# The last tile's way out: quantisation on two engines, down product in two column halves, stores on two queues

## The reference

```python
    x = x + ffn(cond(x, length, log_dt, C, log_A_real, A_imag, D), w_gate, w_up, w_down, ...)

    def cond(u, ...):                        # a convolution, written with FFTs
        u_m = u * mask[:, None, :]
        y = irfft(rfft(u_m, n=1024) * rfft(kernel, n=1024))[..., :512]
        return (y + u_m * D[:, None]) * mask[:, None, :]

    def ffn(x, ...):
        xq = int4_quant(x)                   # mean |x| of a row, round, clip to -8..7
        gate = bitlinear(xq, w_gate, s_gate) # 512 -> 1376
        up = bitlinear(xq, w_up, s_up)       # 512 -> 1376
        gate = jnp.square(jax.nn.relu(gate))
        inter = int8_quant(up * gate)        # max |x| of a row, x * 127 / (gamma + eps), round
        return bitlinear(inter, w_down, s_down)   # 1376 -> 512
```

## Time and profile before

| | |
|---|---|
| median of 3 runs | 215.71 us (215.28 to 215.75) |
| the profiled execution | 215.85 us |
| its span, from the first to the last instruction | 214.1 us |
| mean granted TensorE clock | 0.991 of full speed (2.4 GHz) |
| TensorE, VectorE, ScalarE busy | 84%, 78%, 54% of the span |
| the last add ends, the last store is issued | 210.7 us, 211.2 us |

### The profile page before, as it was taken

The page is one execution under the profiler, slowest core; times in us unless marked ns, Lnnn a source line. Parts: engine busy times, 40 slices in busy tenths (PEclk is TensorE's granted clock), DMA queues, the critical chain, the costliest instruction groups (busy, mean ns, idle before and its releaser), DMA issues.

```text
span 214.1 us, 3425 instructions
## 1 busy us (share of the span) xinstructions
PE 180.8 (84%) x1136; PEld 97.0 (45%) x1136; DVE 168.0 (78%) x457; ACT 115.0 (54%) x184; POOL 11.0 (5%) x29
## 2 busy tenths in 40 slices
PE   1011679499969999999999999999999999998882
PEld 1011576345524554545454545454545545454340
DVE  5999886579987979696968787786969696969841
ACT  2277949829943645545463728282736455464410
POOL 4034502000000000000000000000000000000000
PEclk9999999969999999999999999999999999999999
DMA  3999849426999676667483949484757667070722
GB/s 79 370 385 307 283 122 336 140 74 170 168 202 227 189 162 195 146 169 175 139 213 118 221 116 225 114 243 91 227 116 203 126 190 150 15 164 5 165 49 49
DMA packets 43488, 36.61 MB, mean 171 GB/s; under 512 B 29872, under 2 KB 29952, under 8 KB 43472
## 3 DMA queue, kind: packets, MB, share of 16 engines
q1 hardware_dynamic: 42816, 34.93, 62.6%
q10 hardware_dynamic: 336, 1.41, 1.9%
q0 software_dynamic: 320, 0.06, 0.3%
HBM read 25.27 MB, written 4.28 MB: 138 GB/s over the span
## 4 chain that ended last, share of the span: by engine, by line
PE 71%; DVE 11%; ACT 8%; issue 3%; DMA 3%; SPq 2%; DVEq 0%
PE down_ps L607 18%; PE gate_ps L566 16%; PE up_ps L571 15%; PE conv_ps L481 15%; PE tr_act_ps L471 2%; DMA int_gate<-int_down 2%; ACT int_up L642 2%; PE tr_dve_ps L494 1%; ACT int_gate L649 1%; ACT int_down L642 1%; ACT int_up L649 1%; DVE inter L1046 1%; PE tr_dve_ps L536 1%; DMA c_in<-in_L_cond_C_dram 1%; SPq L358 1%
## 5 line engine op out<-in xcount | busy, mean ns | idle before, releaser
L705 ACT ACTIVATE g<-gate_ps,gu_scale 128x416 f32<-128x416 f32 (+2 forms) x48 | 30.5, 636 | 66.5 <-issue 55.6
L1046 DVE SCALAR_TENSOR_TENSOR inter<-up_ps,gu_scale,g 128x416 f32<-128x416 f32 (+2 forms) x48 | 33.1, 690 | 18.3 <-ACT g L708 18.2
L566 PE MATMUL gate_ps<-gate_t,q_t 128*128 128x416 bf16 (+2 forms) x192 | 45.2, 358 | 1.1 <-DVE q_t L985 1.1
L571 PE MATMUL up_ps<-up_t,q_t 128*128 128x416 bf16 (+2 forms) x192 | 45.5, 360 | 0.0
L607 PE MATMUL down_ps<-down_t,i_t 128*128 128x512 bf16 (+1 forms) x176 | 40.7, 380 | 2.2 <-DVE i_t L1073 1.0
L481 PE MATMUL conv_ps<-toep,x_t 128*64 128x512 f32 (+3 forms) x256 | 39.1, 449 | 0.1
L1050 DVE TENSOR_REDUCE imax<-inter 128x1 f32<-128x416 f32 (+2 forms) x48 | 30.3, 631 | 1.6
L708 ACT ACTIVATE g<-g 128x416 f32<-128x416 f32 (+2 forms) x48 | 28.1, 586 | 1.5
L571 PEld LDWEIGHTS up_ps<-up_t,q_t 128*128 128x128 bf16 x192 | 18.8, 98 | 18.5 <-issue 0.2
L607 PEld LDWEIGHTS down_ps<-down_t,i_t 128*128 128x128 bf16 (+1 forms) x176 | 17.0, 98 | 22.4 <-DVE i_t L1073 1.4
L481 PEld LDWEIGHTS conv_ps<-toep,x_t 128*64 128x64 f32 x256 | 17.2, 139 | 20.7 <-issue 16.8
(11 more groups left out here) (170 smaller groups left out, 165.4 us busy)
## 6 DMA issues: line engine op xcount, KB each, us to landing
toep<-k_back SPq DMA_DIRECT2D x16, 512.0 KB, 5.1
x_in<-in_x_dram SPq DMA_DIRECT2D x32, 128.0 KB, 2.8
x_res<-in_x_dram SPq DMA_DIRECT2D x32, 128.0 KB, 4.0
out_dram<-o_sb SPq DMA_DIRECT2D x32, 128.0 KB, 2.5
raw_gate<-in_L_ffn_w_gate_dram SPq DMA_DIRECT2D x1, 1536.0 KB, 7.2
raw_up<-in_L_ffn_w_up_dram SPq DMA_DIRECT2D x1, 1536.0 KB, 13.9
raw_down<-in_L_ffn_w_down_dram ACTq DMA_DIRECT2D x1, 1376.0 KB, 6.9
raw_down<-in_L_ffn_w_down_dram SPq DMA_DIRECT2D x1, 1376.0 KB, 9.0
```

Of the source, the lines that this page charges most:

```text
L566: mm = pe.matmul(gate_ps[bank][:, 0:cn], q_t[p][:, i, :], gate_t[:, i, c0:c0 + cn], start=(i == 0), stop=(i == KB - 1))
L571: mm = pe.matmul(up_ps[bank][:, 0:cn], q_t[p][:, i, :], up_t[:, i, c0:c0 + cn], start=(i == 0), stop=(i == KB - 1))
L705: nc.scalar.activation(g2[bank][:, 0:cn], gate_ps[bank][:, 0:cn], ACT.Relu, scale=gu_scale[p][:, 0:1]).then_inc(relu_done, 1)
L1046: v.scalar_tensor_tensor(out=inter[:, c0:c0 + cn], in0=up_ps[bank][:, 0:cn], scalar=gu_scale[p][:, 1:2], in1=g2[bank][:, 0:cn], op0=ALU.mu ...
```

## The change

It concerns the last tile alone, and the add of the one before:

- ScalarE quantises the 608 columns, VectorE the 768 as before; both wait for `iscale`, for which there is a new semaphore `iscale_ready`.
- `keep_clock(8)` becomes `keep_clock(2)`.
- The shares of the copies change hands: VectorE copies the first six blocks, ScalarE the other five, in two instructions.
- The down product runs twice over the eleven blocks, for output columns 0 to 255 into `conv_ps` and for 256 to 511 into `up_ps[0]`. It waits for VectorE's copy, and before block seven for ScalarE's. It no longer waits for tile 14's add.
- VectorE adds tile 14 behind its copy, and then each half as it is done (`add_out`).
- SyncE stores the first half in two DMAs (64 rows of 1 KB each) and then half 0 of the second; ScalarE issues the DMA of the second's other 64 rows.

```diff
+        LAST = [(conv_ps, slice(0, L // 2)), (up_ps[0], slice(L // 2, L))]
 # SyncE
-                if k >= 2:
+                if k == T + 1:
+                    sp.wait_ge(out_ready, T)
+                    for half in range(2):
+                        sp.dma_start(in_dram(out, T - 1, half)[:, LAST[0][1]],
+                                     o_sb[p][half_rows(half), LAST[0][1]]).then_inc(stored[p], 16)
+                    sp.wait_ge(out_ready, T + 1)
+                    sp.dma_start(in_dram(out, T - 1, 0)[:, LAST[1][1]],
+                                 o_sb[p][half_rows(0), LAST[1][1]]).then_inc(stored[p], 16)
+                elif k >= 2:
 # TensorE, turn_last
-                keep_clock(8)
+                keep_clock(2)
 # TensorE, down
                 if k == T:
-                    pe.wait_ge(it_act_copied, 1)
+                    pe.wait_ge(it_dve_copied, T)
+                    for bank, cols in LAST:
+                        for c in range(IB):
+                            if c == IT_SPLIT:
+                                pe.wait_ge(it_act_copied, 1)
+                            r = P if c < IB - 1 else IR
+                            mm = pe.matmul(bank[:, 0:L // 2], i_t[0:r, c, :], down_t[0:r, c, cols],
+                                           start=(c == 0), stop=(c == IB - 1))
+                        mm.then_inc(down_done, 1)
+                    return
 # ScalarE
                 if k == T:
-                    act.wait_ge(it_turned, 1)
+                    act.wait_ge(iscale_ready, 1)
+                    act.wait_ge(it_loaded, 16 * (T - 1))
+                    cut = slice(IT_SPLIT * P, I)
+                    nc.scalar.activation(inter_q[:, cut], inter[:, cut], ACT.Copy,
+                                         scale=iscale[:]).then_inc(inter_quant, 1)
+                    act.wait_ge(it_turned, 2)
                     act.wait_ge(down_done, T - 1)
-                    nc.scalar.copy(i_t[:, 0:IT_SPLIT, :].rearrange("p c t -> p (c t)"),
-                                   tr_act_ps[:, 0:IT_SPLIT * P // 2].bitcast(I16)).then_inc(it_act_copied, 1)
+                    nb = IB - 1 - IT_SPLIT
+                    nc.scalar.copy(i_t[:, IT_SPLIT:IB - 1, :].rearrange("p c t -> p (c t)"),
+                                   tr_dve_ps[:, 0:nb * P // 2].bitcast(I16))
+                    nc.scalar.copy(i_t[0:IR, IB - 1, :], tr_dve_ps[0:IR, nb * P // 2:(nb + 1) * P // 2].bitcast(I16)
+                                   ).then_inc(it_act_copied, 1)
+                    act.wait_ge(out_ready, T + 1)
+                    act.dma_start(in_dram(out, T - 1, 1)[:, LAST[1][1]],
+                                  o_sb[1][half_rows(1), LAST[1][1]]).then_inc(stored[1], 16)
 # VectorE
+                def add_out(n, bank, cols, done):
+                    q = n % 2
+                    dve.wait_ge(down_done, done)
+                    dve.wait_ge(res_loaded[q], 32 * (n // 2 + 1))
+                    wait(dve, stored[q], 32 * (n // 2))
+                    v.scalar_tensor_tensor(out=o_sb[q][:, cols], in0=bank[:, 0:cols.stop - cols.start],
+                                           scalar=oscale[q][:], in1=x_res[q][:, cols],
+                                           op0=ALU.mult, op1=ALU.add).then_inc(out_ready, 1)
...
                 if k == T:
-                    dve.wait_ge(it_turned, 2)
+                    dve.wait_ge(it_turned, 1)
                     dve.wait_ge(down_done, T - 1)
-                    nb = IB - 1 - IT_SPLIT
-                    v.tensor_copy(i_t[:, IT_SPLIT:IB - 1, :].rearrange("p c t -> p (c t)"),
-                                  tr_dve_ps[:, 0:nb * P // 2].bitcast(I16))
-                    v.tensor_copy(i_t[0:IR, IB - 1, :], tr_dve_ps[0:IR, nb * P // 2:(nb + 1) * P // 2].bitcast(I16)
-                                  ).then_inc(it_dve_copied, 1)
+                    v.tensor_copy(i_t[:, 0:IT_SPLIT, :].rearrange("p c t -> p (c t)"),
+                                  tr_act_ps[:, 0:IT_SPLIT * P // 2].bitcast(I16)).then_inc(it_dve_copied, 1)
+                    add_out(T - 2, down_ps, slice(0, L), T - 1)
+                    for h, (bank, cols) in enumerate(LAST):
+                        add_out(T - 1, bank, cols, T + h)
...
+                        v.reciprocal(iscale[:], gam127[:]).then_inc(iscale_ready, 1)
+                        dve.wait_ge(iscale_ready, 1)
                         dve.wait_ge(it_loaded, 16 * (T - 1))
-                        for cut, ready in ((slice(0, IT_SPLIT * P), last_quant), (slice(IT_SPLIT * P, I), inter_quant)):
-                            v.tensor_scalar(inter_q[:, cut], inter[:, cut], iscale[:], None,
-                                            ALU.mult).then_inc(ready, 1)
+                        cut = slice(0, IT_SPLIT * P)
+                        v.tensor_scalar(inter_q[:, cut], inter[:, cut], iscale[:], None,
+                                        ALU.mult).then_inc(last_quant, 1)
```

More of the change, by code:

```diff
@@ L226, in adaln_ffn @@
         last_quant = sem("last_quant")
+        iscale_ready = sem("iscale_ready")
         it_turned = sem("it_turned")
@@ L383, in _ @@
             for p in range(2):
-                sp.wait_ge(stored[p], 32 * (T // 2))
+                sp.wait_ge(stored[p], 32 * (T // 2 + p))
         @block.gpsimd
@@ L596, in down @@
                 if k == T:
-                    pe.wait_ge(it_act_copied, 1)
-                else:
-                    pe.wait_ge(it_dve_copied, m)
+                    pe.wait_ge(it_dve_copied, T)
[8 more added lines that the diff above has]
+                    return
+                pe.wait_ge(it_dve_copied, m)
                 if k == 1:
@@ L603, in down @@
                 for c in range(IB):
-                    if c == IT_SPLIT and k == T:
-                        pe.wait_ge(it_dve_copied, m)
                     r = P if c < IB - 1 else IR
@@ L1098, in body @@
                     step(v.tensor_scalar(gam127[:], gamma[:], EPS, 1.0 / 127.0, ALU.add, ALU.mult))
-                    step(v.reciprocal(iscale[:], gam127[:]))
                     if k != T - 1:
+                        step(v.reciprocal(iscale[:], gam127[:]))
                         if k >= 1:
@@ L1106, in body @@
                     else:
+                        v.reciprocal(iscale[:], gam127[:]).then_inc(iscale_ready, 1)
+                        dve.wait_ge(iscale_ready, 1)
                         dve.wait_ge(it_loaded, 16 * (T - 1))
-                        for cut, ready in ((slice(0, IT_SPLIT * P), last_quant), (slice(IT_SPLIT * P, I), inter_quant)):
-                            v.tensor_scalar(inter_q[:, cut], inter[:, cut], iscale[:], None,
-                                            ALU.mult).then_inc(ready, 1)
+                        cut = slice(0, IT_SPLIT * P)
+                        v.tensor_scalar(inter_q[:, cut], inter[:, cut], iscale[:], None,
+                                        ALU.mult).then_inc(last_quant, 1)
                 if k == 1:
                     y_mask(3)
[L1114 to L1122, removed]
+                if 1 <= k < T - 1:
+                    add_out(m - 1, down_ps, slice(0, L), m)
                 if k < T - 2 and k != 1:
```

## The result

The changed kernel takes 213.1 us as the median of 15 runs (211.05 to 213.37), the kernel before, measured beside it, 215.28 us (213.64 to 215.75). The ratio is 0.989, with a 95% interval of 0.9861 to 0.9918. The prediction was 213.2.

The account below looks back on a forecast made before the run. The prediction took one serial chain from tile 14's down product to bound the end: 1.30 + 0.23 + 0.26 + 0.70 = 2.49 us off 215.85 is 213.36, less 0.14 for the median, 213.2 us; range 212.7 to 214.3.

Parts of the forecast that it names:

- The bound: From tile 14's down product on, one serial chain without overlap; whatever is taken out moves the end by as much.
- Six identity matmuls: Before the last tile's transposes: two instead of eight let the first transpose start 1.30 us earlier, at 204.63.
- Quantisation on two engines: Last tile's second 608 columns on ScalarE: the gain of 0.3 us is hidden behind the transposes, so 0.
- the 0.7 to 0.75: Sign to see in the changed trace: ScalarE's 608 columns take 0.7 to 0.75 us, ended before the seventh transpose.
- the cover of 0.46: Slack between ScalarE's quantisation ending at 204.50 and the second group of transposes, which cannot start before 204.96.
- Shares of the copies: VectorE copying the first six blocks: 0.66 us from transposes' end to first down matmul, where it was 0.89; -0.23.
- Down in halves: Last down product as 22 matmuls of 256 columns for eleven of 512: 2.52 us as now, loads hidden; 0.
- the rival of +1.2: Half-width down matmuls are paced by their weight loads: +1.2 us, hence 214.4; chance 0.05.
- The last add: VectorE's add of the second half, 256 columns: 0.49 us, from 208.38 to 208.87; -0.26.
- The stores: Last two stores, halved and on two queues: issue and transfer give -0.73, containing the issue's 0.50; taken as -0.70 us.
- 0.15 for a halved store: By the Trainium skill's DMA fit, halving a 128 KB store at the end would give an estimated 0.15 us.
- The clock: Rival: with less filler TensorE's clock falls from 2.4 to 1.2 GHz in the last tile, 216.3 us; chance 0.04.

Follow-up runs that it names:

- a_dveq: The changed kernel with both pieces of the quantisation on VectorE; 213.31 us in one run, span end 8.13 us after the last RECIPROCAL's start, for 8.10.

## Why the prediction was right

- **The bound.** What was taken out of the last tile's chain came off its end: 1.77 us by the last add for a forecast of 1.79.
- **Six identity matmuls.** 1.30 forecast; 1.30 measured by removing them alone and by putting them back. The largest term, and it needed only one row: the filler was the last thing before the transposes while their data were ready.
- **Quantisation on two engines.** Forecast nothing, measured nothing (a_dveq). ScalarE's 608 columns took 0.80 where I had worked out 0.73: the price from weights of 2560 and 3072 columns was 0.07 low, outside the 0.7 to 0.75 that the prediction gave as a sign, and the cover of 0.46 took it.
- **Shares of the copies.** -0.23 forecast, 0.23 measured at the add. ScalarE's copies ended 0.25 before they were needed, not 0.13, because its two instructions overlap (0.74 together, not 0.87).
- **Down in halves.** Forecast nothing; 2.59 from first start to last end for 2.55 in one piece, since each of the 22 costs some 0.0025 beyond its columns (they start 0.109 apart, where 256 columns at 2.4 GHz are 0.1067). Loads stayed hidden, the rival of +1.2 is out.
- **The last add.** -0.26 forecast, 0.744 to 0.48 measured. The working has a slip: 0.744 for 512 columns and 0.676 for 448 make 1.06 ns a column, not 0.97, and 0.47 for 256, not 0.49.
- **The stores.** -0.70 forecast, -0.65 measured, but the working behind it was put together wrongly, and that the sum came out is partly luck. I gave 0.50 to the issue and the rest to the data. The issue is worth 0.26 to 0.40, since stores from two queues share the DMA engines and land 0.2 to 0.3 later; the halves are worth 0.25 to 0.39, and not 0.2. The Trainium skill ("DMA: Bandwidth & Descriptors", Issuing engines are not separate DMA queues) lets a second queue save only the issue time. The saving measured is no more than that: 0.40 of the 0.59 between two issues of 64 KB, 0.26 of the 0.50 between two of 128 KB. That two queues moved the 256 KB in 1.1 us for 1.35 doesn't go against it: whether they flowed faster because the second store was issued sooner or for another reason was not tried, and from one queue too the DMA engines' busy share was 0.82 to 1.01 in the four windows from 212.00 to 213.00. The prediction's 0.15 for a halved store rests on a fit that the Trainium skill (the same page, Anatomy of one DMA) gives for DMAs issued by GpSimd. These are issued by SyncE and ScalarE, and here 64 KB landed 0.3 sooner than 128 KB (2.0 and 2.3).
- **The clock.** It did not fall in the last tile, in any of the twelve traces, with eight, two or no filler matmuls.

The profiled pair differs by 3.2 us of span, and 0.76 of that is not the change's: it was there by the first tile, and the clock fell in both. Taken from the medians the gain is 2.2 us, for 2.49 forecast; the interval of the ratio contains both, and the medians mix executions with and without the fall of the clock. Taken like with like it is 2.4: the executions with a mean clock of 0.989 to 0.992, as both profiled ones have, take 215.5 us in the mean of 36 before and 213.1 in the mean of 11 changed. That the time itself, 213.1, came within 0.1 of 213.2 is partly luck: the kernel before, measured again, had a median of 215.28 and not the 215.71 that I had subtracted from, and the smaller gain made up for it.

## What to carry to other kernels

Filler that keeps TensorE's clock up belongs where the trace shows an idle stretch followed by a fall, not on the chain: here eight matmuls at the end cost 1.3 + 0.18 us for nothing, and ten in the first tile's gap kept off a fall that costs 1.5 us in the executions that have it. When runs of one kernel spread wider than the effect, measure from an event just ahead of the change to the end of the span, and find the stretch in which the spread arises. Price each part of an edit by the cover it has: of the six parts here, the one that stands first in the title was worth nothing.

## What was not expected of the hardware

- Two stores issued together from two queues moved 256 KB in about 1.1 us, with 369 GB/s in one quarter of a microsecond; issued 0.50 apart from one queue the same bytes took about 1.35 us at some 200 GB/s.
- A store of 64 KB landed 2.0 us after its issue, one of 48 KB 1.9 and one of 128 KB 2.3; issued from ScalarE beside one from SyncE 2.2 to 2.3, 2.1 and 2.6.
- TensorE's clock fell in the first tile in eight of ten traces, where it had idled 2.3 to 2.6 us, and not in the two where it had idled 1.6, and this alone spread the times of one kernel by some 1.5 us.
